# Layer 0 attention: attend and both projections as fp32 matmuls of unsplit operands, in place of products of fp16 pairs

## What is computed

```python
qh = _split_heads(q @ w_q.T + b_q)          # q is the normalised x
kh = _split_heads(k @ w_k.T + b_k)          # k and v are the context
vh = _split_heads(v @ w_v.T + b_v)
scores = jnp.einsum('bhqd,bhkd->bhqk', qh, kh) / jnp.sqrt(jnp.float32(d_k))   # 16 heads of 16
attn = jax.nn.softmax(scores, axis=-1)
out = jnp.einsum('bhqk,bhkd->bhqd', attn, vh)
return out.transpose(0, 2, 1, 3).reshape(B, S, H * d) @ w_o.T + b_o
```

## Time and profile before

| | us |
|---|---|
| median of 3 runs (3129.72 to 3131.92) | 3130.3 |
| span of the profiled execution | 3124.2 |
| PE busy | 2797.3 (90%) |
| DVE busy | 2640.9 (85%) |
| ACT busy | 1875.0 (60%) |
| POOL busy | 2190.1 (70%) |

### The profile page before, as it was taken

One profiled execution on the slowest core, in us unless ns is written; L12 is line 12 of the kernel. 1 busy time (PEld: TensorE's weight loads), 2 busy tenths in 40 slices (PEclk: granted clock), 3 DMA queues, 4 the chain that ended last, 5 costly groups with the idle time before them and its releaser, 6 DMA issues.

```text
span 3124.2 us, 101333 instructions
## 1 busy us (share of the span) xinstructions
PE 2797.3 (90%) x33450; PEld 2225.3 (71%) x33450; DVE 2640.9 (85%) x6703; ACT 1875.0 (60%) x3733; POOL 2190.1 (70%) x3924
## 2 busy tenths in 40 slices
PE   4889896788888888869899999999999999999997
PEld 2444444666666666647688888888888888888886
DVE  6887886888888888875699999998989988999986
ACT  2666765777777777775455545555545555555553
POOL 3892001666667666645488888888888888888887
PEclk9999998999999999989999999999999999999999
DMA  5987666232223222623444444444444344444441
GB/s 153 361 332 289 244 243 227 73 86 79 73 78 83 80 74 77 224 82 81 96 104 111 107 101 95 104 104 95 101 91 97 94 103 104 96 98 93 108 94 43
DMA packets 367621, 388.79 MB, mean 124 GB/s; under 512 B 118432, under 2 KB 341264, under 8 KB 362320
## 3 DMA queue, kind: packets, MB, share of 16 engines
q1 hardware_dynamic: 346960, 335.42, 38.9%
q0 software_dynamic: 7328, 23.40, 2.4%
q10 hardware_dynamic: 12960, 25.23, 2.2%
HBM read 235.08 MB, written 148.83 MB: 123 GB/s over the span
## 4 chain that ended last, share of the span: by engine, by line
PE 39%; DVE 6%; issue 3%; POOL 2%; ACT 2%; DVEq 0%; POOLq 0%; ACTq 0%
PE banks L150 11%; PE banks L152 11%; PE banks L151 10%; PE banks L1310 2%; PE banks L1295 2%; DVE a_probT_lo L1397 1%; PE banks L1342 1%; ACT a_qT_hi L1199 1%; DVE a_pick L1522 1%; DVE a_y L1541 1%; DVE a_rsum L1409 1%; PE banks L1365 1%; DVE a_wsel L1531 0%; PE banks L1357 0%; ACT a_ynT_hi L1199 0%
## 5 line engine op out<-in xcount | busy, mean ns | idle before, releaser
L1199 ACT ACTIVATE a_qT_hi<-banks 128x512 f16<-128x512 f32 x252 | 150.5, 597 | 700.8 <-PE banks L152 700.8
L383 POOL TENSOR_TENSOR a_probT_lo<-a_expT,a_probT_hi 128x512 f16<-128x512 f32 (+1 forms) x384 | 372.0, 998 | 243.7 <-ACT a_probT_hi L458 243.7
L449 ACT ACTIVATE a_expT<-banks,a_top,w_score_scale 128x512 f32<-128x512 f32 (+1 forms) x384 | 272.2, 709 | 111.4 <-PE banks L544 111.2
L1112 POOL TENSOR_TENSOR a_pn<-a_prob,a_rsum 128x1024 f32<-128x1024 f32 (+1 forms) x256 | 307.2, 1221 | 5.8 <-DVE a_rsum L1411 5.3
L150 PE MATMUL banks<-a_xnT_hi,w_q_hi 128*128 128x256 f16 x1024 | 281.6, 275 | 4.7 <-DVE a_xnT_lo L1395 3.0
L150 PE MATMUL banks<-a_vo_front,a_probT_hi 128*128 128x256 f16 x1024 | 278.9, 272 | 2.7 <-DVE a_probT_lo L1397 2.6
L152 PE MATMUL banks<-a_xnT_hi,w_q_lo 128*128 128x256 f16 x1024 | 280.9, 274 | 0.0
L151 PE MATMUL banks<-a_xnT_lo,w_q_hi 128*128 128x256 f16 x1024 | 280.9, 274 | 0.0
L152 PE MATMUL banks<-a_vo_front,a_probT_lo 128*128 128x256 f16 x1024 | 279.0, 273 | 0.0
L151 PE MATMUL banks<-a_vo_front,a_probT_hi 128*128 128x256 f16 x1024 | 279.0, 272 | 0.0
L1397 DVE SCALAR_TENSOR_TENSOR a_probT_lo<-banks,a_probT_hi 128x512 f16<-128x512 f32 (+1 forms) x384 | 212.6, 582 | 35.7 <-ACT a_probT_hi L1199 35.3
(11 more groups left out here) (400 smaller groups left out, 10655.0 us busy)
## 6 DMA issues: line engine op xcount, KB each, us to landing
vo<-kv_vo_out SPq DMA_DIRECT2D x38, 2048.0 KB, 7.6
a_vo_front<-vo SPq DMA_DIRECT2D x128, 512.0 KB
kt<-kv_k_out ACTq DMA_DIRECT2D x9, 2560.0 KB, 15.0
a_k<-kt SPq DMA_DIRECT2D x64, 308.0 KB, 3.5
kv_raw_e<-in_L_ffn_w POOLq DMA_DIRECT2D x16, 1024.0 KB, 9.7
a_x<-in_x SPq DMA_DIRECT2D x64, 256.0 KB
a_y<-in_x SPq DMA_DIRECT2D x64, 256.0 KB, 2.8
x<-a_y SPq DMA_DIRECT2D x64, 256.0 KB, 2.2
```

The lines of the kernel that those rows point to most:

```text
L383: pool.tensor_tensor(probT[b][1][0:rows, first:end, :], expT[b][0:rows, first:end, :], probT[b][0][0:rows, first:end, :], ALU.subtract).th ...
L449: act.activation(expT[1 - h][0:rows, first:end, :], bank, ACT.Exp, bias=top[0:rows, 0:1], scale=weights["score_scale"][0:rows, 0:1]).then_ ...
L1112: last = pool.tensor_tensor(keys_of(pn[h]), keys_of(prob_of(u, h, 2)), rsum[h][:, :].unsqueeze(2).broadcast_to([P, H, n]), ALU.mult)
L1199: act.activation(out, bank[:, 0:cols].rearrange("p (c s) -> p c s", c=out.shape[1]), ACT.Copy, scale=scale)\
```

## The change

`attend`, the projection by w_q and the projection by w_o become fp32 matmuls of unsplit fp32 tiles. `xnT`, `attT`, w_q and w_o are one fp32 tile each; `probT` and the tile of zeros go away and `attend` reads `expT`; `v` is stored and loaded as 17 fp32 values a head (16 and a one) in place of 33 fp16 ones. `attend` begins with the two `back` matmuls. ACT no longer makes `probT` hi, DVE no longer makes the lo halves of the attention and of the normalised rows, POOL no longer makes `probT` lo. Queries and keys stay pairs. In the projection phase the value step is one DVE instruction in place of DVE, ACT, DVE.

```diff
-    xnT = pair("xnT", [P, DC, SEQ])
+    xnT = sb("xnT", [P, DC, SEQ])
-    front = [sb(f"front{p}", [P, 2, 2, MAIN, 2 * head + 1], F16) for p in range(2)]
-    back = [sb(f"back{p}", [MAIN * BACK, 2, 2, MAIN, 2 * head + 1], F16) for p in range(2)]
+    front = [sb(f"front{p}", [P, 2, 2, MAIN, head + 1]) for p in range(2)]
+    back = [sb(f"back{p}", [MAIN * BACK, 2, 2, MAIN, head + 1]) for p in range(2)]
...
-            need(act, prob_ready, (t - 1) * PG)
-            act.activation(expT[1 - h][0:rows, first:end, :], bank, ACT.Exp, bias=top[0:rows, 0:1],
+            need(act, att_ready, t - 1)
+            act.activation(expT[1 - h][0:rows, first:end, :], bank, ACT.Exp,
...
-                        last = matmul3(nc, bank[:, 0:SEQ], [w[:, c, n * P:(n + 1) * P] for w in wq],
-                                       [a[:, c, :] for a in xnT], c == 0, c == DC - 1)
+                        last = nc.tensor.matmul(bank[:, 0:SEQ], wq[:, c, n * P:(n + 1) * P], xnT[:, c, :],
+                                                start=c == 0, stop=c == DC - 1)
...
-            need(pe, prob_ready, (t + 1) * PG)
+            need(pe, exp_done, (t + 1) * PG)
...
-            nc.tensor.matmul(bank[:, 0:COLS], hi[:, 0, :], zero[:, :], start=True, stop=False)
-            for c in range(MAIN):
-                at, value = 2 * c, front[p][:, e, :, c % BLK * (MAIN // BLK) + c // BLK, :]
-                nc.tensor.matmul(out[:, at:at + 2, :], hi[:, c, :], value[:, :, head:], start=False, stop=False)
-                nc.tensor.matmul(out[:, at:at + 2, 0:head], hi[:, c, :], value[:, :, 0:head], start=False, stop=False)
-                nc.tensor.matmul(out[:, at:at + 2, :], lo[:, c, :], value[:, :, head:], start=False, stop=False)
             rows = HEIGHT[2]
             for c in range(2):
...
+                nc.tensor.matmul(out[:, c * MAIN:(c + 1) * MAIN, :], expT[h][0:rows, MAIN + c, :],
+                                 back[p][:, e, c, :, :], start=c == 0, stop=False)
+            for c in range(MAIN):
+                last = nc.tensor.matmul(out[:, 2 * c:2 * c + 2, :], expT[h][:, c, :],
+                                        front[p][:, e, :, c % BLK * (MAIN // BLK) + c // BLK, :],
+                                        start=False, stop=c == MAIN - 1)
...
-                        last = matmul3(nc, bank[:, 0:D], [a[:, c, :] for a in attT], [w[:, c, :] for w in wo], c == 0,
-                                       c == DC - 1)
+                        last = nc.tensor.matmul(bank[:, 0:D], attT[:, c, :], wo[:, c, :], start=c == 0,
+                                                stop=c == DC - 1)
...
-                nc.vector.tensor_tensor(v_sum[0:m, :], full(g, ("v", a))[0:m, 0:D], bv[0:m, :], ALU.add)\
-                    .then_inc(v_sum_ready, 1)
-                need(dve, v_hi, at + 1)
-                need(dve, v_sum_ready, at + 1)
-                nc.vector.tensor_tensor(v_out[p][0:m, a, :, :, 0:D // H], by_head(v_sum[0:m, :]),
-                                        v_out[p][0:m, a, :, :, D // H:2 * (D // H)], ALU.subtract).then_inc(v_ready, 1)
+                nc.vector.tensor_tensor(v_out[p][0:m, a, :, :, 0:D // H], by_head(full(g, ("v", a))[0:m, 0:D]),
+                                        by_head(bv[0:m, :]), ALU.add).then_inc(v_ready, 1)
```

More of the change, by code:

```diff
@@ L375, in add_row @@
                 .then_inc(row_added, 1)
[L377 to L384, removed]
         def body(i, u, j):
@@ L430, in prepare @@
                 if use[0] == "xnT":
-                    act.activation(xnT[0][:, n, :], bank, ACT.Copy).then_inc(xnT_hi, 1)
+                    act.activation(xnT[:, n, :], bank, ACT.Copy).then_inc(xnT_ready, 1)
                 else:
@@ L551, in attend @@
             p, e = u // 2, u % 2
-            need(pe, prob_ready, (t + 1) * PG)
+            need(pe, exp_done, (t + 1) * PG)
             need(pe, v_in[p], (j + 1) * V_LOADS)
-            hi, lo = probT[h]
             bank = bank_for(i, ("att", h))
             out = bank[:, 0:COLS].rearrange("p (h d) -> p h d", h=H)
-            nc.tensor.matmul(bank[:, 0:COLS], hi[:, 0, :], zero[:, :], start=True, stop=False)
-            for c in range(MAIN):
-                at, value = 2 * c, front[p][:, e, :, c % BLK * (MAIN // BLK) + c // BLK, :]
-                nc.tensor.matmul(out[:, at:at + 2, :], hi[:, c, :], value[:, :, head:], start=False, stop=False)
-                nc.tensor.matmul(out[:, at:at + 2, 0:head], hi[:, c, :], value[:, :, 0:head], start=False, stop=False)
-                nc.tensor.matmul(out[:, at:at + 2, :], lo[:, c, :], value[:, :, head:], start=False, stop=False)
             rows = HEIGHT[2]
             for c in range(2):
-                at, value, n = c * MAIN, back[p][:, e, c, :, :], MAIN + c
-                nc.tensor.matmul(out[:, at:at + MAIN, :], hi[0:rows, n, :], value[:, :, head:], start=False, stop=False)
-                nc.tensor.matmul(out[:, at:at + MAIN, 0:head], hi[0:rows, n, :], value[:, :, 0:head], start=False,
-                                 stop=False)
-                last = nc.tensor.matmul(out[:, at:at + MAIN, :], lo[0:rows, n, :], value[:, :, head:], start=False,
-                                        stop=c == 1)
+                nc.tensor.matmul(out[:, c * MAIN:(c + 1) * MAIN, :], expT[h][0:rows, MAIN + c, :],
[4 more added lines that the diff above has]
+                                        start=False, stop=c == MAIN - 1)
             filled(last, i, ("att", h))
@@ L1855, in keys_values_phase @@
     rowsT = [pair(f"rowsT{p}", [P, DC, BANK]) for p in range(2)]
-    v_out = [sb(f"v_out{p}", [P, CH, 2, H // 2, 2 * (D // H) + 1], F16) for p in range(2)]
+    v_out = [sb(f"v_out{p}", [P, CH, 2, H // 2, D // H + 1]) for p in range(2)]
     v_ones = sem("v_ones")
@@ L2173, in body @@
                 turn(g, 1 - p)
-            for a, m in enumerate(chunks(g)):
-                need(act, v_sum_ready, g * CH + a + 1)
-                act.activation(v_out[p][0:m, a, :, :, D // H:2 * (D // H)], by_head(v_sum[0:m, :]), ACT.Copy)\
-                    .then_inc(v_hi, 1)
         first_scalar(act)
@@ L2184, in _ @@
         act.wait_ge(inverse0_ready, 1)
-        for n, parts in enumerate(turned0):
-            split16(nc, True, parts[0][:, :, :], parts[1][:, :, :],
-                    full(GROUPS - 1, ("w0", n)).rearrange("p (c o) -> p c o", c=DC), inverse0[:, n:n + 1], hi0_done, n + 1,
-                    lo0_done)
+        for n, tile in enumerate(turned0):
+            act.activation(tile[:, :, :], full(GROUPS - 1, ("w0", n)).rearrange("p (c o) -> p c o", c=DC), ACT.Copy,
+                           scale=inverse0[:, n:n + 1])
     @block.vector
@@ L2290, in _ @@
         groups(dve, body)
[L2291 to L2294 removed]
 def layer0_weights(nc, ctx):
     sb = lambda n, s, d=FP32: ctx.enter_context(nc.sbuf_tensor(f"w0_{n}", s, d))
[L2301 to L2302 removed]
+    return {"q": sb("qT", [P, DC, D]), "o": sb("oT", [P, DC, D]), "q_bias": sb("bq", [P, DC]), "rows": (sb("bo", [P, D]), sb("bo_ffn", [P, D])),
             "score_scale": sb("score_scale", [P, 1]), "out_scale": sb("y_scale", [P, 1])}
```

68 lines of the change are left out of this document (16 added, 52 removed).

## The result

| | before | after |
|---|---|---|
| median of 4 runs each | 3130.0 us (3127.4 to 3131.9) | 3166.9 us (3165.3 to 3170.1) |
| ratio, 95% interval | | 1.0124 (1.011 to 1.0139) |
| span of the profiled execution | 3124.2 | 3166.0 |
| PE busy | 2797.3 (90%) | 2970.6 (94%) |
| DVE busy | 2640.9 (85%) | 2553.1 (81%) |

A forecast was written before the change was run, and what follows sets the result against it. PE was to become the pace-setter of the attention phase, at 12.75 us a batch for 12.11. +40 for batches, −2.7, −2 and +1 at the edges gave +36: span 3160, median 3166 us, range 3132 to 3214.

The forecast's parts named there:

- I carry this over: Last step of the sum: the runs' median stands 6.1 us above the profiled span, so 3160 becomes 3166 us.
- Rival 1: Narrow fp32 passes in `attend` are cheaper in a dense run, so the kernel gains; at 0.06 us a pass, 3060; chance 0.06.
- rival 3: PE's weight loads are not hidden behind the stream: a batch takes 16.3 us, the kernel 3390; chance 0.03.
- 12.30 of work and 0.45 of waiting: PE's attention batch after the change: 12.75 us in all, +0.64 a batch, +40 us over 62 batches.
- group 2: Transposes on PE that still wait for the exponential of group 0 when h = 0, about 0.3 us.
- rival 4: PE is granted 1.2 GHz for a quarter of the attention phase: 14.6 us a batch, 3283; chance 0.06.
- busy near 9.0: DVE's work in an attention batch: 10.7 us less 1.7 for four instructions taken off, of a 12.75 us batch.
- None of this is a gain by itself: Savings a batch on DVE (1.7 us), ACT (at least 2.5) and POOL (at least 4.6) only end PE's waits, 2.90 us.
- So this stretch runs at 1.2 GHz: Program's start: transposes 0.22 us apart, twice 0.11, so its 1.6 ns a column becomes 0.81 at 2.4 GHz.
- (a): End of the projection phase: the last group's shorter value step lets its store leave earlier, −2.7 us.
- (b): The end: PE's 1.96 us wait goes, the last two `attend` cost 2.3 more, two lo halves go; −2 us.
- (c): The start: four projections' matmuls at half clock cost 3.4 us in place of 2.6, one DVE step goes; +1 at most.

The follow-up runs named there:

- the two runs that loaded DVE and unloaded PE: The changed kernel with two spare DVE subtractions a tile, 3163.7 us; the changed kernel with four of eight narrow `attend` matmuls left out in every tile, 3055.3 us.
- twice the columns: The changed kernel with each narrow matmul of `attend` streaming 68 columns in place of 34: 3165.3 us.
- both projections alone: The kernel before with only the w_q and w_o projections as fp32 matmuls, `attend` and v staying pairs: 3056.5 us, 0.9775 of before.
- w_q alone: The kernel before with only the projection by w_q as fp32 matmuls; w_o, `attend` and v stay pairs: 3064.6 us.
- w_o alone: The kernel before with only the output projection by w_o as fp32 matmuls: 3128.7 us.
- run with w_q alone and two spare subtractions: The kernel before with only the w_q projection in fp32, plus two spare 256-column DVE subtractions a batch where the rows' lo halves stood: 3127.4 us.
- The spare statistics: The kernel before with only the w_q projection in fp32, plus two spare single-operand DVE row statistics a batch where the rows' lo halves stood: 3102.6 us.

## Why the prediction was right, point by point

- **The sum for the span: 3160 forecast, 3166.0 measured. The median: 3166 forecast, 3166.9 measured.** The second agreement is partly luck. I took the 6.1 us between span and median for what lies around the span. In the ten experiments with one run it is 1.7 (3064.6 for a span of 3062.9, 3162.7 for 3161.0), and at 0.9 in the kernel after. So the profiled execution of before was itself some 4 us faster than its median. The step "I carry this over" failed by 5, and the sum by 6 the other way. Of these 6, 3 lie in the batches (+43.1 for +40: 12.80 for 12.75, and the batch of before is 12.09 over all 61, not 12.11), the rest at the edges (−1.3 for −3.7).
- **PE becomes the engine that sets the pace: shown**, by 400.00 of 400 and by the two runs that loaded DVE and unloaded PE.
- **A pass costs the larger of 0.113 and 0.83 ns × columns: held.** `attend` 2.18 and 2.23 for 2.26; a w_q projection 0.86 for 0.85; twice the columns at the same price; 0.112 by leaving matmuls out. Rival 1 fell with it, and rival 3.
- **12.30 of work and 0.45 of waiting: 12.80 measured for 12.75, by two errors that nearly cancel.** `attend` and projections took 4.41 + 3.81 = 8.22 where 7.92 was forecast, the 0.37 at the two w_o projections in it; the rest 4.59 where 4.38 was, with the 0.31 of group 2 in it, the one wait that I had said would stay. Without these two, work is 12.81 − 0.68 = 12.13, 0.17 less than forecast, and 0.68 of standing still is 0.23 more. The waits for `att` and for all lo halves of rows and attention went, as forecast.
- **The clock (rival 4): 1.00 from 800 to 1200 us**, in every run.
- **DVE "busy near 9.0": 9.9** (309.49 / 400 × 12.80). The four instructions were taken off at 0.42 each, but in the kernel before they stood in a queue where records overlap: L693 starts at 917.72 and the next instruction at 918.05, so such a one fills 0.33. That explains 0.36 of the 0.9. With both projections alone, where the same four are gone, DVE is busy 346.97 / 400 × 10.90 = 9.45; the other 0.45 came with `attend` and was not traced. It decided nothing here.
- **"None of this is a gain by itself" was wrong as a reading of before.** It held for the sum, since PE's new work covers the saving. But taking the lo half of the rows off DVE, work and wait for ACT's copy together, gained 1.00 us a batch (w_q alone), while the same number of instructions gained nothing where the wait stayed (w_o alone).
- **"So this stretch runs at 1.2 GHz"** rested on the pace of transposes alone: the granted clock reads 1.00 from 7 to 15 us. The changed kernel has narrow passes where it reads 0.50, which is 1.2 GHz, from 551 to 554 us: 16 of them stand 551.36 to 554.75, 0.212 apart, against 0.107 at 909.64. So halving the start's price for full clock was right.
- **Edges.** (a) −2.7 forecast: the three value steps and the store of the last group took 1.09 where they took 4.11, −3.0, as forecast. The last group's first value step also stood 5.5 earlier. How much of that is the change's, one pair of runs can't tell: with the old step it stands anywhere from 509.7 to 515.2 in nine profiled runs, with the new one from 508.2 to 513.5 in five. At the first statistics 5.5 of the 8.5 were left; there the nine stand at 528.8 on average and the five at 526.1, the 2.7 that was forecast. (b) −2 forecast, +1.1 measured: behind the last maximum shown four `attend` are still to come, not two, each about 1.1 dearer, while one wait of 1.96 and the lo halves go. (c) +1 forecast, +2.1 measured: the first `attend` waited 2.06 for the transfer of `back`, and from 540 to 567 us the granted clock was 0.68, where the same stretch of the kernel before (540 to 571) had 0.74. Which of the two made the difference, no run tells.

The first `attend` of the kernel after:

```profile
550.32 1.24 PE L530 MATMUL banks<-a_back,a_expT 104*128 104x136 f32 x4 [2.06 <-DMA a_back<-v]
551.36 3.46 PE L533 MATMUL banks<-a_front,a_expT 128*128 128x34 f32 x16
554.75 0.44 PE L502 MATMUL banks<-a_k,a_qT_hi 32*128 32x154 f16 x8
```

## What to carry to other kernels

Replacing a split product by an fp32 one trades matmuls for passes, so decide it by the moving width: at 256 columns six fp16 matmuls cost 0.66 us and the four passes of two fp32 ones 0.86, and the work of making lo halves on other engines falls away; at 34 columns two passes cost 0.224 and three fp16 matmuls 0.078, and the split wins by far. Change such places one by one: here the whole made the kernel 1.2% slower and one part alone makes it 2.2% faster.

Before you call a saving on a busy engine worthless, look at what stands in its queue ahead of the instruction that others wait for, and at what that stands waiting for itself. Here taking out an instruction together with its wait gained 1.00 us a batch; taking out equal work in front of that wait gained nothing; and a step of 0.15 us that waits cost as much as the work of 0.42. The instruction to take out or to move need not be one that the waiting engine's waits name.

## What I had not expected of the hardware

The same subtraction of 256 columns with both operands in SBUF took DVE 417 ns in the changed kernel, where POOL is 20% busy (L655 above), and 676 ns where POOL is 69% busy, half of the time with subtractions (run with w_q alone and two spare subtractions):

```profile
L624 DVE TENSOR_TENSOR a_spare<-a_spare_in 128x256 f16<-128x256 f32 x66 | 44.6, 676 | 0.0
```

The spare statistics, with one operand, took 418 ns in the same place, with POOL 71% busy. ACT's exponential of 512 columns went from 780 to 690 ns when its bias operand and POOL's subtractions went; which of the two it was, no run tells. The Trainium skill, "GPSIMD Engine Reference", section Specifications, says that POOL contends with DVE instructions that have two SBUF inputs; the rows agree. So the run with the spare subtractions put 1.35 us a batch on DVE, not 0.84, and the one with statistics is the cleaner test.
